# A transformer block with causal attention: shift rows and normalised outputs made by other engines, and TensorE's row halves taken in turn

## The chip, the cores and the metric

The kernel runs on one core of a Trainium2 chip. The metric is the device time of one execution in microseconds (us); the median of three runs of the kernel before is 739.92 us (739.89 to 741.77). A core has five engines that run their own instruction lists in order and meet by semaphores: TensorE (PE in the rows; PEld is its weight loading), VectorE (DVE), ScalarE (ACT), GpSimd (POOL) and SyncE (SP, which issues most transfers here). PSUM, where TensorE writes, has eight banks.

## The reference

For `x` of 4 x 1024 x 128:

```
x = x + 0.5 * ffn(layernorm(x))          # 8 experts of 64, 2 chosen, and a shared one
x = x + attention(layernorm(x))          # 16 heads of 8, 4 key heads, causal, slope bias
x = x + 0.5 * ffn(layernorm(x))
scores = q @ k.T * 8**-0.5 + slope * (key - query)     # -inf where key > query
out = softmax(scores) @ v
```

## The kernel before, in words

The first feed-forward part runs over 8 groups of 512 tokens; then comes attention in 16 **units** (one batch with one key head, four query heads), then the output projection (`out_proj`) and the second feed-forward part. The change lies in the attention and at its start and end.

A unit does two passes. **Pass 1** finds each query's largest score, so that the exponentials of pass 2 don't overflow. It is cut into 38 **pieces** (`PIECES`, numbered 0 to 37 here as in the code). A piece is one PSUM bank of scores with queries on the partitions: one product of up to 512 keys, or, where the causal part is narrow, a **merged** piece of two or four products and two products that add the causal mask (`per` over 1). Heads 0 and 1 of a unit lie on partitions 0 to 63, heads 2 and 3 on 64 to 127, so each product uses 57 or 59 rows of one **half** of the array. Even pieces use one half, odd pieces the other. VectorE reduces each piece to its maxima (`reduce`, L903, or L894 and L896 where a mask is added). The pieces go through a **ring** of three PSUM banks (`RING`): TensorE may write piece n only when what lay three places before it in the ring has been read (`slot`).

When pieces 0 to 11 are reduced, and again when all 38 are, `maxima` (L914) makes two bf16 rows from the 16 maxima per partition: the negative of the maximum, rounded, and what the rounding lost. TensorE transposes them (`maxima_T`, L1172, its row in the trace is L1175), VectorE copies them out (`rows_out`, L907), and SyncE moves them beside the queries (`load_maxima`), where they subtract the maximum as two more rows of the product.

**Pass 2** has 12 **steps** (one block of 128 keys with 512 queries). For each step TensorE makes scores with keys on the partitions (`score`, two head slots of two heads, one on each half of the array, and masks on the diagonal), ScalarE takes the exponential (`attention` of ACT, L624), and two steps later (`LAG`) TensorE multiplies by the values and a column of ones (`times_v`), four heads beside one another in bank `OBANK`. After 4 and after 12 steps ScalarE copies that bank out (`out_evac`, L613), TensorE transposes it back into the ring (`out_T`, L1178, helper L1023), and VectorE divides by the sum of the row (`normalise`, L935: a reciprocal, L940, and a multiplication, L941).

Pass 1 of unit i+1 runs between the steps of unit i. The order on TensorE is written by hand: `PER_STEP[s]` says how many pieces stand before the scores of step s+1, behind each of its two head slots, and behind `times_v`; `maxima_T(i, 1)` stands at the end of step 0, `out_T(i-1, 1)` of step 4, `maxima_T(i+1, 0)` of step 5, `out_T(i, 0)` of step 6. VectorE takes everything in the same order as the ring. GpSimd has little to do in attention: `load_v` (L520) once per unit and `add_bo` (L514) in the first eight. In the last unit there is no pass 1.

Of the kernel before, what the change touches and what calls it, by code (L numbers as in the profile page):

```python
# [8 lines left out]
ALU = mybir.AluOpType  # L9
# [3 lines left out]
P = 128  # L13
# [56 lines left out]
PER_STEP = [(2, 1, 0, 0), (0, 1, 1, 0), (0, 2, 2, 1), (0, 2, 0, 0), (0, 3, 0, 0), (0, 2, 0, 1),  # L70
# [11 lines left out]
LAG, PR_BUFS = 2, 5  # L82

# [92 lines left out]
def macaron(nc, dram, out):  # L176
    ctx = ExitStack()
    with ctx:
# [26 lines left out]
        mhalf = sb("mhalf", [P, GT])  # L205
        wg = sb("wg", [P, HT, P])
# [49 lines left out]
        mm_ = sb("mm_", [P, QT, HPG])  # L256
        wb = sb("wb", [P, 2, 2, SLOTS, QT], BF16)
# [3 lines left out]
        rden = sb("rden", [P, QT * HPG])  # L261
        attn = sb("attn", [P, UNITS, SEQ // P, HPG * DH])
# [52 lines left out]
        a_w = sem("a_w")  # L315
        a_wc = sem("a_wc")
# [4 lines left out]
        a_ov = sem("a_ov")  # L321
        a_on = sem("a_on")
# [141 lines left out]
        def _(pool):  # L464
            pool.memset(mhalf[:, :], -0.5)
            pool.memset(ones[:, :], 1.0)
# [54 lines left out]

            def values_and_bo(i, par, first, last):
                if not last:
                    load_v(i + 1, 1 - par)
                if i < BO_PARTS:
                    add_bo(i)

            pool.wait_ge(f1.v, GROUPS)
            load_v(0, 0)
            over_units(values_and_bo)  # L530
# [7 lines left out]
        def _(act):  # L538
# [75 lines left out]

            def attention():
# [16 lines left out]
                out_evac(UNITS - 1, 1)  # L632

# [17 lines left out]
        def _(dve):  # L651
# [231 lines left out]
            def reduce(i, n):  # L883
                t, h, per, k0, w, diag = PIECES[n]
                done = NP1 * i + n + 1
                b, at = ring.take(a_out, done)
# [18 lines left out]
            links = Chain(dve, a_ch)  # L905

# [7 lines left out]
            def maxima(i, j):  # L914

                dve.wait_ge(a_out, NP1 * i + (NP1 if j else FIRST_HALF))
                m = mx[:, 0, 0]
                if j:
                    m = mm_[:, :, :]
                    links.link(dve.tensor_tensor(m, mx[:, 1, 0], mx[:, 1, 1], V.max))  # L920
                after(dve, a_wc, 2 * i + j)
                m = m.rearrange("p t (r s) -> p r s t", r=2)
                links.link(dve.tensor_scalar(wb[:, :, 0, :, :], m, -1.0, None, V.mult))  # L923
                dve.scalar_tensor_tensor(out=wb[:, :, 1, :, :], in0=m, scalar=-1.0, in1=wb[:, :, 0, :, :],
                                         op0=V.mult, op1=V.subtract).then_inc(a_w, 1)

            def early_maxima(some):

                for n in some:
                    reduce(0, n)  # L930
                    if n == FIRST_HALF - 1:
                        maxima(0, 0)

            def attention(last_split):
                def normalise(i, j):  # L935
                    b, at = ring.take(a_on, 2 * i + j + 1)
                    after(dve, a_on, 2 * i + j)
                    dve.wait_ge(a_in, at + 1)
                    o = bank(b).rearrange("p (m e) -> p m e", m=QT * HPG)
                    links.link(dve.reciprocal(rden[:, :], o[:, :, DH]))  # L940
                    dve.tensor_tensor(  # L941
                        attn[:, i, QT * j:QT * j + QT, :].rearrange("p t (h d) -> p (t h) d", h=HPG),
                        o[:, :, 0:DH], rden[:, :, None].broadcast_to([P, QT * HPG, DH]), V.mult)\
                       .then_inc(a_on, 1)

# [4 lines left out]
                maxima(0, 1)  # L950
                START_LINKS = 3
                UNIT_LINKS = 2 + 3

                def body(i, par, first, last):

                    links.at(START_LINKS + UNIT_LINKS * i - (0 if first else 1))
                    for s in range(NSTEP):
                        if not last:
                            for n in range(part(s, 0).start, part(s, 3).stop):
                                reduce(i + 1, n)  # L960
                                if n == FIRST_HALF - 1:
                                    maxima(i + 1, 0)
                        if s == W1_STEP:
                            rows_out(i, par, 1)
                        if s == OT1_STEP and not first:
                            normalise(i - 1, 1)
                        if s == OT0_STEP:
                            normalise(i, 0)
                        if s == W0_STEP and not last:
                            rows_out(i + 1, 1 - par, 0)  # L970
                    if not last:
                        maxima(i + 1, 1)

                over_units(body)
                normalise(UNITS - 1, 1)
# [40 lines left out]
        def _(pe):  # L1016
# [63 lines left out]
            def ffn_down(f, qkv):  # L1080
                def early_pieces(some):
                    for n in some:
                        if n == 0:
                            pe.wait_ge(a_ld[0][0], 16 * LOADS)
                            pe.wait_ge(s_ks0, 4)
                        if n == SECOND_STACK:
                            pe.wait_ge(a_ld[1][0], 16 * LOADS)
                        piece(0, n)
# [65 lines left out]
            def piece(i, n):  # L1154
# [4 lines left out]
                b = slot(a_out, NP1 * i + n + 1)  # L1159
                for k in range(per):  # L1160
                    half, h = k // SLOTS, h0 % SLOTS + k % SLOTS
                    q0, key0 = (t + QT * half) * P, k0 + HALF * half
                    ins = mm(ps[:, b, k * w:k * w + w], qs[at:at + K1, par, q0 // HALF, h, q0 % HALF:q0 % HALF + P],
                             ks[at:at + K1, par, key0:key0 + w], start=k == 0, stop=per == 1)
                if per > 1:
                    o = ps[:, b, 0:per * w].rearrange("p (s n) -> p s n", s=per)
                    mask = mask_qk[at:at + RG, :, None, :].broadcast_to([RG, 2, per, P])
                    mm(o[:, :, w - P:w], spread[at:at + RG, 0, :], mask[:, 0], start=False)
                    ins = mm(o[:, :, w - RG:w], spread[at:at + RG, 1, :], mask[:, 1, :, RG:P], start=False)
                ins.then_inc(a_in, 1)  # L1170

# [187 lines left out]
```

## Time and profile before

| | |
|---|---|
| median of the runs | 739.92 us |
| the profiled execution's own time, and its span | 740.43 us, 738.6 us |
| PE busy, PEld busy | 702.6 us (95%), 365.6 us (50%) |
| DVE busy | 582.3 us (79%) |
| ACT busy, POOL busy | 403.3 us (55%), 112.6 us (15%) |
| the page's chain that ended last | PE 52%; DVE 13%; issue 11%; ACT 2% |
| TensorE's granted clock, mean | 0.972 |

Attention's full units lie between about 190 and 575 us of the span, the last one up to 600. Shares are averages over stages with different limits, so the units are read by themselves. In a timeline a row is one or more like instructions of one engine: start, length, what they are, how many, and in brackets how long the engine sat idle before and what released it. Records overlap where an engine is pipelined.

### The profile page before, as it was taken

Reading aid. Unit: us, or ns where it says so; the run is one execution under the profiler, and the core shown is the slowest. Engines: PE = TensorE matmul, PEld = TensorE weight load, DVE = VectorE, ACT = ScalarE, POOL = GpSimd, SP = SyncE. Lnnn points to the kernel's source line nnn. Section 1 sums busy time; section 2 is a strip of 40 time slices with the busy share of each in tenths; the row PEclk is TensorE's granted clock in tenths of the full one; section 3 lists DMA queues with packets and bytes.
Section 4 is the critical chain, followed back from the end, with each engine's and each line's share of the span. In section 5 each row is a group of like instructions: output and inputs, shape, how many; then the busy total and the mean of one; then the engine's idle time right before and its main releaser. Section 6 shows DMA issues by size and latency. Waiting matters only on the chain.

```text
span 738.6 us, 15927 instructions
## 1 busy us (share of the span) xinstructions
PE 702.6 (95%) x5906; PEld 365.6 (50%) x5906; DVE 582.3 (79%) x1921; ACT 403.3 (55%) x579; POOL 112.6 (15%) x122
## 2 busy tenths in 40 slices
PE   8999998967999999999999999999999889999998
PEld 4554487833344444444444444444444255554598
DVE  6976468697999999999999999999999238766311
ACT  3353332132667777776777777677777743353300
POOL 3202882110000000000000000000000002103950
PEclk9999999975899999999999999999999999999999
DMA  8014533442010011001100100110010000005531
GB/s 217 1 16 77 93 64 113 144 139 85 25 38 26 27 26 40 20 21 38 33 26 20 39 20 22 39 38 20 21 39 1 2 1 0 2 1 91 107 92 58
DMA packets 47249, 34.69 MB, mean 47 GB/s; under 512 B 13106, under 2 KB 46514, under 8 KB 47172
## 3 DMA queue, kind: packets, MB, share of 16 engines
q1 hardware_dynamic: 46596, 33.60, 18.6%
q8 instruction: 47, 0.77, 0.4%
q14 instruction: 30, 0.25, 0.1%
q10 hardware_dynamic: 576, 0.08, 0.1%
HBM read 23.01 MB, written 10.39 MB: 45 GB/s over the span
## 4 chain that ended last, share of the span: by engine, by line
PE 52%; DVE 13%; issue 11%; ACT 2%; DVEq 0%; ACTq 0%
PE ps L1018 49%; DVE mx L903 8%; PE ps L1023 4%; DVE mx L896 1%; ACT h_all L624 1%; DVE h_all L896 1%; DVE xn L705 1%; DVE stats L693 0%; DVE wb L923 0%; DVE mm_ L920 0%; DVE sg L838 0%; ACT osb L613 0%; DVE idle L894 0%; DVEq L133 0%; DVE mv L697 0%
## 5 line engine op out<-in xcount | busy, mean ns | idle before, releaser
L624 ACT ACTIVATE h_all<-ps 128x1024 f32<-128x1024 f32 (+3 forms) x384 | 291.3, 810 | 112.4 <-PE ps L1018 109.2
L903 DVE TENSOR_REDUCE mx<-ps 128x1 f32<-128x512 f32 (+2 forms) x352 | 223.0, 681 | 9.2 <-PE ps L1018 5.8
L1018 PE MATMUL ps<-ks,xnT_all 57*128 57x512 bf16 (+3 forms) x768 | 178.9, 337 | 15.6 <-DVE mx L896 6.4
L1018 PE MATMUL ps<-h_all,vb 128*32 128x512 f32 (+3 forms) x1536 | 163.8, 500 | 0.6 <-ACT osb L613 0.6
L1018 PE MATMUL ps<-xnT_all,ks 59*128 59x512 bf16 (+3 forms) x768 | 158.6, 331 | 3.6 <-ACT h_all L624 3.4
L896 DVE CUSTOM_DVE_ANT_0 h_all<-ps,mask_w 128x384 bf16<-128x384 f32 (+1 forms) x256 | 149.3, 618 | 2.3 <-issue 0.7
L1018 PEld LDWEIGHTS ps<-ks,xnT_all 57*128 57x128 bf16 x768 | 56.5, 94 | 143.4 <-DVE mx L896 64.9
L1018 PE MATMUL ps<-cb 64*128 64x64 bf16 (+3 forms) x1216 | 113.0, 215 | 0.0
L717 DVE TENSOR_TENSOR h_all<-ps,sg 128x512 f32<-128x512 f32 x80 | 55.2, 690 | 50.5 <-PE ps L1018 48.8
L563 ACT ACTIVATE sg<-ps 128x512 f32<-128x512 f32 x80 | 47.8, 597 | 82.6 <-PE ps L1018 82.3
L1018 PEld LDWEIGHTS ps<-cb 64*128 64x128 bf16 x1216 | 80.1, 96 | 17.3 <-issue 0.7
L1018 PE MATMUL ps<-xnT_all,wg 128*128 128x512 f32 x160 | 83.3, 602 | 0.0
L1018 PE MATMUL ps<-xnT_all,wu 128*128 128x512 f32 x160 | 81.7, 592 | 0.0
L1018 PE MATMUL ps<-wds,h_all 128*128 128x128 f32 x640 | 76.0, 279 | 0.0
L1018 PEld LDWEIGHTS ps<-wds,h_all 128*128 128x128 f32 x640 | 74.0, 194 | 2.7 <-issue 2.7
L1018 PEld LDWEIGHTS ps<-xnT_all,ks 59*128 59x128 bf16 x768 | 45.0, 93 | 42.8 <-ACT h_all L624 26.0
L520 POOL COPY vb<-v_all 128x64 f32<-128x64 f32 x16 | 3.7, 238 | 376.4 <-PE ps L1018 362.0
L1018 PEld LDWEIGHTS ps<-h_all,vb 128*32 128x32 f32 x1536 | 30.5, 108 | 38.1 <-issue 29.2
L1018 PEld LDWEIGHTS ps<-xnT_all,wu 128*128 128x128 f32 x160 | 30.4, 190 | 38.3 <-issue 38.0
L480 POOL TENSOR_TENSOR rstd<-ve,mhalf 128x4 f32<-128x4 f32 x24 | 24.2, 1009 | 151.6 <-DVE ve L699 145.0
L1018 PEld LDWEIGHTS ps<-xnT_all,wg 128*128 128x128 f32 x160 | 28.9, 190 | 28.7 <-issue 28.7
L858 DVE TENSOR_TENSOR x<-x,ps 128x512 f32<-128x512 f32 x16 | 10.9, 683 | 34.0 <-PE ps L1018 34.0
(120 smaller groups left out, 553.6 us busy)
## 6 DMA issues: line engine op xcount, KB each, us to landing
xnT_all<-q_scr SPq DMA_DIRECT2D x64, 96.0 KB
attn<-sel_scr SPq DMA_DIRECT2D x12, 256.0 KB, 7.2
mask_second<-sel_scr SPq DMA_DIRECT2D x12, 256.0 KB, 8.2
q_scr<-qp SPq DMA_DIRECT2D x8, 384.0 KB
ks<-k_scr SPq DMA_DIRECT2D x64, 48.0 KB
x<-in_x SPq DMA_DIRECT2D x8, 256.0 KB, 5.7
yT<-sel_scr SPq DMA_DIRECT2D x8, 256.0 KB, 9.0
q_scr<-qp SPq DMA_DIRECT2D x8, 256.0 KB
```

Source lines behind the costliest of these rows:

```text
L480: pool.tensor_tensor(rstd[:, par, :], ve[:, par, :], mhalf[:, :], ALU.pow).then_inc(rs_sem, 1)
L520: pool.tensor_copy(vb[:, par, :, 0:DH], v_all[:, i, :, :]).then_inc(a_vb, 1)
L563: act.activation(sg[:, b, :], bank(3 + b), ACT.Silu).then_inc(f.sg, 1)
L624: act.activation(pr[:, (NSTEP * i + s) % PR_BUFS, p:HPG:SLOTS, lo:HALF], ps[:, b:b + 2, lo:HALF], ACT.Exp)\
L705: ins = dve.tensor_scalar(xn[:, t, :], x[:, c * GT + t, :], mv[:, par, t, 0:1], rstd[:, par, t:t + 1], V.subtract, V.mult)
L717: dve.tensor_tensor(h_all[:, TILE_ORDER[k][0], TILE_ORDER[k][1], :], bank(5 + b), sg[:, b, :], V.mult)\
L858: dve.tensor_tensor(xt(c), xt(c), y, V.add).then_inc(f.x, 1)
L896: dve.tensor_tensor_reduce(out=junk, in0=ps[:, b, 0:w], in1=mask_w[:, HALF - w:HALF], scale=1.0, scalar=LOWEST, op0=V.add, op1=V.max, accu ...
L903: dve.tensor_reduce(m, src, AX.X, V.max).then_inc(a_out, 1)
L1018: return pe.matmul(o, l, r, start=start, stop=stop, skip_group_check=True)
L1023: ins = pe.transpose(ps[:, b, t * P:(t + 1) * P], src(t), ident)
```

## The change

- `maxima` leaves VectorE. GpSimd makes the rows (`shift_rows`: a multiplication by -1, a copy to bf16, a subtraction). For the second half VectorE still takes the maximum of two sets (`second_maxima`).
- `normalise` leaves VectorE. ScalarE copies 9 columns of each of 16 groups from the ring's bank to `raw` (`out_copy`, in steps 5 and 7, after the second exponential), and GpSimd raises the sums to the power -1 and multiplies. ScalarE's copy now empties that bank of the ring.
- Two merged pieces that stand next to one another in one group are issued as a pair (`two_pieces`): both banks are waited for first, then the products alternate between the halves of the array.
- The scores of a step begin with the half that the piece before them did not use.
- `PER_STEP[5]` changes, so that pieces 16 and 17 stand together, behind `times_v`.
- `maxima_T`, `out_T` and the steps keep their places.

```diff
-PER_STEP = [..., (0, 2, 0, 1),
+PER_STEP = [..., (0, 1, 0, 2),
...
@@ GpSimd
+            def normalise(i, j):
+                n = 2 * i + j + 1
+                pool.wait_ge(a_oc, n)
+                pool.tensor_tensor(rden[:, :], raw[:, j, :, DH], mone[:, :], ALU.pow).then_inc(a_rd, 1)
+                pool.wait_ge(a_rd, n)
+                pool.tensor_tensor(attn[...], raw[:, j, :, 0:DH], rden[...].broadcast_to(...), ALU.mult).then_inc(a_on, 1)
+                pool.wait_ge(a_on, n)
             def values_and_bo(i, par, first, last):
                 if not last:
                     load_v(i + 1, 1 - par)
                 if i < BO_PARTS:
                     add_bo(i)
+                if not last:
+                    shift_rows(i + 1, 0)
+                if not first:
+                    normalise(i - 1, 1)
+                normalise(i, 0)
+                if not last:
+                    shift_rows(i + 1, 1)
+                else:
+                    normalise(i, 1)
+            def shift_rows(i, j):
+                links = 2 * (2 * i + j)
+                m = mx[:, 0, 0]
+                if j:
+                    pool.wait_ge(a_mm, i + 1)
+                    m = mm_[:, :, :]
+                else:
+                    pool.wait_ge(a_out, NP1 * i + FIRST_HALF)
+                after(pool, a_wc, 2 * i + j)
+                pool.tensor_tensor(nm[:, :, :], m, mone.rearrange(...), ALU.mult).then_inc(a_nm, 1)
+                pool.wait_ge(a_nm, links + 1)
+                less = nm.rearrange("p t (r s) -> p r s t", r=2)
+                pool.tensor_copy(wb[:, :, 0, :, :], less).then_inc(a_nm, 1)
+                pool.wait_ge(a_nm, links + 2)
+                pool.tensor_tensor(wb[:, :, 1, :, :], less, wb[:, :, 0, :, :], ALU.subtract).then_inc(a_w, 1)
...
@@ ScalarE
+            def out_copy(i, j):
+                n = turned[i, j]
+                act.wait_ge(a_in, n)
+                after(act, a_on, 2 * i + j - 1)
+                act.activation(raw[:, j, :, :], bank((n - 1) % RING)...[:, :, 0:DH + 1], copy).then_inc(a_oc, 1)
...
+                            if p == 1 and s == OT1_STEP + 1 and not first:
+                                out_copy(i - 1, 1)
+                            if p == 1 and s == OT0_STEP + 1:
+                                out_copy(i, 0)
...
@@ VectorE
-            def maxima(i, j):
-                ...
-                def normalise(i, j):
-                    ...
+            def second_maxima(i):
+                dve.wait_ge(a_out, NP1 * (i + 1))
+                after(dve, a_w, 2 * i)
+                dve.tensor_tensor(mm_[:, :, :], mx[:, 1, 0], mx[:, 1, 1], V.max).then_inc(a_mm, 1)
...
@@ TensorE
+            def two_pieces(i, n):
+                upper, lower = slot(a_out, NP1 * i + n + 1), slot(a_out, NP1 * i + n + 2)
+                for first, second in zip(piece_products(i, n, upper), piece_products(i, n + 1, lower)):
+                    pass
+                first.then_inc(a_in, 1)
+                second.then_inc(a_in, 1)
+                RowsUsed.last = PIECES[n + 1][1] // SLOTS
...
             def score(i, s, p, par):
-                for r in range(2):
+                order = (1 - RowsUsed.last, RowsUsed.last)
+                for r in order:
```

How instructions move at the three places of which the prediction speaks:

TensorE, step 5 of a unit. `xnT_all,ks` are scores of pass 2, `ks,xnT_all` products of pieces, `cb` the mask products of a merged piece, `h_all,vb` is `times_v`, `cb,wb` is `maxima_T`. Before:

```order
L1018 MATMUL ps<-xnT_all,ks 128x512 x2
L1018 MATMUL ps<-ks,xnT_all 128x512
L1018 MATMUL ps<-ks,xnT_all 128x256 x2
L1018 MATMUL ps<-cb 128x2x128
L1018 MATMUL ps<-cb 128x2x64
L1018 MATMUL ps<-xnT_all,ks 128x512 x2
L1018 MATMUL ps<-h_all,vb 32x128 x4
L1018 MATMUL ps<-ks,xnT_all 128x256 x2
L1018 MATMUL ps<-cb 128x2x128
L1018 MATMUL ps<-cb 128x2x64
L1175 MATMUL ps<-cb,wb 32x128
```

And with the change:

```order
L1072 MATMUL ps<-xnT_all,ks 128x512 x2
L1072 MATMUL ps<-ks,xnT_all 128x512
L1072 MATMUL ps<-xnT_all,ks 128x512 x2
L1072 MATMUL ps<-h_all,vb 32x128 x4
L1072 MATMUL ps<-ks,xnT_all 128x256 x4
L1072 MATMUL ps<-cb 128x2x128 x2
L1072 MATMUL ps<-cb 128x2x64 x2
L1257 MATMUL ps<-cb,wb 32x128
```

Piece 16 has moved from before the second scores and `times_v` to behind them, and its five instructions alternate with those of piece 17.

VectorE, from piece 10 to piece 17 of a unit (steps 3 to 5), where `maxima` and `normalise` stood. Before:

```order
L903 TENSOR_REDUCE mx<-ps 128x2x2 [waits a_in] x2
L923 TENSOR_SCALAR wb<-mx 128x2x8 [waits a_wc,a_out]
L924 SCALAR_TENSOR_TENSOR wb<-mx,wb 128x2x8 [waits a_ch]
L903 TENSOR_REDUCE mx<-ps 128x1 [waits a_in] x3
L940 RECIPROCAL rden<-ps 128x16 [waits a_in,a_on]
L941 TENSOR_TENSOR attn<-ps,rden 128x128 [waits a_ch]
L903 TENSOR_REDUCE mx<-ps 128x1 [waits a_in]
L903 TENSOR_REDUCE mx<-ps 128x2 [waits a_in] x2
L912 COPY wt<-ps 32x128 [waits a_wd_first,a_in]
```

And with the change:

```order
L985 TENSOR_REDUCE mx<-ps 128x2x2 [waits a_in] x2
L985 TENSOR_REDUCE mx<-ps 128x1 [waits a_in] x4
L985 TENSOR_REDUCE mx<-ps 128x2 [waits a_in] x2
L992 COPY wt<-ps 32x128 [waits a_wd_first,a_in]
```

The reduces of pieces 10 to 17 now follow one another with nothing between.

GpSimd, one of the first eight units. Before:

```order
L520 COPY vb<-v_all 128x8x8 [waits a_pv]
L514 TENSOR_TENSOR x<-x,bo 128x512
```

And with the change:

```order
L541 TENSOR_TENSOR x<-x,bo 128x512
L585 TENSOR_TENSOR nm<-mx,mone 128x16 [waits a_wc,a_out]
L588 CAST wb<-nm 128x2x8 [waits a_nm]
L590 TENSOR_TENSOR wb<-nm,wb 128x2x8 [waits a_nm]
L553 TENSOR_TENSOR rden<-raw,mone 128x16 [waits a_oc]
L555 TENSOR_TENSOR attn<-raw,rden 128x128 [waits a_rd]
L553 TENSOR_TENSOR rden<-raw,mone 128x16 [waits a_oc,a_on]
L555 TENSOR_TENSOR attn<-raw,rden 128x128 [waits a_rd]
L585 TENSOR_TENSOR nm<-mm_,mone 128x16 [waits a_wc,a_mm,a_on]
L588 CAST wb<-nm 128x2x8 [waits a_nm]
L590 TENSOR_TENSOR wb<-nm,wb 128x2x8 [waits a_nm]
```

GpSimd has ten instructions more per unit, in one line with the two that it had.

## Rows read from the trace of the kernel before

**Rows 1.** Busy time by engine, units 1 to 7 (length, PE, PEld, DVE, ACT, POOL, clock, DMA):

```profile
199.60:399.50 199.90, 196.40 (x2174) 85.35 (x2175) 192.23 (x630) 149.08 (x205) 10.43 (x15) 1.00 0.11 29
```

**Rows 2.** The instructions on tile mm_: one per unit, ns min/median/max, first and last start:

```profile
L920 DVE TENSOR_TENSOR mm_<-mx x16: 174/175/176, 189.3 to 574.9; 128x16 f32<-128x16 f32 x16
```

**Rows 3.** Timeline of DVE: a wait, then piece 0, piece 12 of the next unit:

```profile
310.16 1.89 DVE L903 TENSOR_REDUCE mx<-ps 128x1 f32<-128x512 f32 x3 [0.28 <-PE ps L1018]
...
317.88 0.17 DVE L920 TENSOR_TENSOR mm_<-mx 128x16 f32<-128x16 f32 x1
...
318.40 1.28 DVE L903 TENSOR_REDUCE mx<-ps 128x2 f32<-128x512 f32 x2
...
325.66 0.17 DVE L923 TENSOR_SCALAR wb<-mx 128x16 bf16<-128x16 f32 x1
...
326.14 1.29 DVE L903 TENSOR_REDUCE mx<-ps 128x1 f32<-128x512 f32 x2
```

**Rows 4.** The chain that ended last, one unit (start, length, what):

```profile
321.37 0.03 DVE h_all L896
...
321.99 5.12 PE ps L1018 x46
...
329.74 0.70 DVE mx L903
...
330.49 2.37 PE ps L1018 x14
```

**Rows 5.** Timeline of PE: pieces 0 and 1, maxima_T, pieces 5 and 6, pieces 12 to 14:

```profile
317.52 0.40 PE L1018 MATMUL ps<-ks,xnT_all 57*128 57x256 bf16 x4
...
319.13 0.23 PE L1175 MATMUL ps<-cb,wb 128*32 128x128 bf16 x1
...
321.00 0.38 PE L1018 MATMUL ps<-ks,xnT_all 57*128 57x512 bf16 x2
...
325.73 0.59 PE L1018 MATMUL ps<-ks,xnT_all 57*128 57x512 bf16 x3
```

**Rows 6.** Timeline of PE, step 5: times_v, the start of piece 17:

```profile
328.79 0.43 PE L1018 MATMUL ps<-h_all,vb 128*32 128x128 f32 x8
329.15 0.39 PE L1018 MATMUL ps<-ks,xnT_all 57*128 57x256 bf16 x2
```

**Rows 7.** Timeline of DVE, steps 4 and 5: normalise, pieces 15 to 17:

```profile
327.95 0.25 DVE L940 RECIPROCAL rden<-ps 128x16 f32<-128x16 f32 x1
...
328.44 2.00 DVE L903 TENSOR_REDUCE mx<-ps 128x1 f32<-128x512 f32 x3
```

**Rows 8.** Groups by line and shape, ACT in attention (busy us, mean ns, idle before):

```profile
L624 ACT ACTIVATE h_all<-ps 128x256 f32<-128x256 f32 x60 | 21.5, 384 | 15.6 <-PE ps L1018 15.5
```

**Rows 9.** Timeline of ACT, exponentials of steps 6 and 8, which follow the two copies:

```profile
328.12 1.02 ACT L624 ACTIVATE h_all<-ps 128x1024 f32<-128x1024 f32 x1 [0.19 <-PE ps L1018]
...
334.11 1.03 ACT L624 ACTIVATE h_all<-ps 128x1024 f32<-128x1024 f32 x1 [1.48 <-PE ps L1018]
```

**Rows 10.** Groups by line and shape, POOL in the whole program:

```profile
L480 POOL TENSOR_TENSOR rstd<-ve,mhalf 128x4 f32<-128x4 f32 x24 | 24.2, 1009 | 151.6 <-DVE ve L699 145.0 <-issue 6.6
...
L514 POOL TENSOR_TENSOR x<-x,bo 128x512 f32<-128x512 f32 x8 | 10.1, 1264 | 0.0
...
L1353 POOL MEMSET const-float32-1.0<- 128x1 f32 x1 | 0.1, 99 | 0.0
```

**Rows 11.** Timeline, all engines, end of attention:

```profile
600.02 0.26 DVE L940 RECIPROCAL rden<-ps 128x16 f32<-128x16 f32 x1 [9.25 <-PE ps L1023]
...
600.73 0.76 DVE L982 COPY sg<-attn 128x512 f32<-128x512 f32 x2
...
601.21 1.09 PE L1023 MATMUL ps<-c,sg 128*128 128x128 f32 x8 [1.30 <-DVE sg L982]
```

**Rows 12.** Busy time by engine, start of the output projection:

```profile
601.20:604.00 2.80, 2.54 (x21) 2.30 (x22) 0.97 (x3) 1.09 (x2) 0.00 (x0) 1.00 0.00 0
```

**Rows 13.** Busy time by engine where TensorE waits for VectorE before attention (the clock is third from last):

```profile
164.00:191.30 27.30, 20.25 (x84) 8.22 (x84) 22.20 (x64) 6.34 (x9) 1.63 (x3) 0.50 0.25 75
```

More of the change, by code:

```diff
@@ L82, with turned_outputs @@
 LAG, PR_BUFS = 2, 5
+def turned_outputs():
+    n = NP1 + 1
+    numbers = {}
+    for i in range(UNITS):
+        for s in range(NSTEP):
+            n += sum(PER_STEP[s]) if i + 1 < UNITS else 0
+            n += s == W1_STEP
+            if s == OT1_STEP and i > 0:
+                numbers[i - 1, 1] = n = n + 1
+            if s == OT0_STEP:
+                numbers[i, 0] = n = n + 1
+            n += s == W0_STEP and i + 1 < UNITS
+    numbers[UNITS - 1, 1] = n + 1
+    return numbers
 BO_PARTS = 8
@@ L261, in macaron @@
         rden = sb("rden", [P, QT * HPG])
+        raw = sb("raw", [P, 2, QT * HPG, DH + 1])
         attn = sb("attn", [P, UNITS, SEQ // P, HPG * DH])
@@ L613, in out_evac @@
                 act.activation(osb[:, j, :], bank(OBANK), copy).then_inc(a_ov, 1)
+            turned = turned_outputs()
+            def out_copy(i, j):
+                n = turned[i, j]
+                act.wait_ge(a_in, n)
+                after(act, a_on, 2 * i + j - 1)
+                act.activation(raw[:, j, :, :], bank((n - 1) % RING).rearrange("p (m e) -> p m e", m=QT * HPG)[:, :, 0:DH + 1],
+                               copy).then_inc(a_oc, 1)
             def attention():
@@ L885, in reduce @@
                 done = NP1 * i + n + 1
+                if n == 0:
+                    after(dve, a_w, 2 * i - 1)
                 b, at = ring.take(a_out, done)
@@ L965, in body @@
                         if s == OT1_STEP and not first:
-                            normalise(i - 1, 1)
+                            ring.take(a_oc, 2 * i)
                         if s == OT0_STEP:
-                            normalise(i, 0)
+                            ring.take(a_oc, 2 * i + 1)
                         if s == W0_STEP and not last:
@@ L1081, in early_pieces @@
                 def early_pieces(some):
[L1082 to L1088, printed above, removed]
+                    if 0 in some:
+                        pe.wait_ge(a_ld[0][0], 16 * LOADS)
+                        pe.wait_ge(s_ks0, 4)
+                    if SECOND_STACK in some:
+                        pe.wait_ge(a_ld[1][0], 16 * LOADS)
+                    pieces_of(0, some)
                 def down(c, par, transpose=False):
@@ L1152, in slot, with piece_products @@
                 return b
-            def piece(i, n):
+            class RowsUsed:
+                last = 1
+            def piece_products(i, n, b):
                 t, h0, per, k0, w, diag = PIECES[n]
@@ L1194, in score @@
                     for half, w in enumerate((RG, P)):
-                        for r in range(2):
+                        for r in order:
                             rows = slice(RG * r, RG * r + RG)
@@ L1221, in attention @@
                 pe.wait_ge(a_ld[1][0], 16 * LOADS)
-                for n in range(EARLY_END + sum(TAIL), NP1):
-                    piece(0, n)
+                pieces_of(0, range(EARLY_END + sum(TAIL), NP1))
                 pe.wait_ge(a_wd[0], 32)
@@ L1229, in pieces @@
                     def pieces(s, k):
-                        for n in () if last else part(s, k):
-                            if n == 0:
-                                next_stack(i, par, 0)
-                            if n == SECOND_STACK:
-                                next_stack(i, par, 1)
-                            piece(i + 1, n)
+                        some = range(0) if last else part(s, k)
+                        if 0 in some:
+                            next_stack(i, par, 0)
+                        if SECOND_STACK in some:
+                            next_stack(i, par, 1)
+                        pieces_of(i + 1, some)
                     for s in range(NSTEP):
```

71 lines of the change are left out of this document (35 added, 36 removed).

## The prediction

> **What bounds the kernel now.** I read the busy shares first, stage by stage. In units 1 to 7 VectorE is busy 192.23 of 199.90 us, 96%, with TensorE's clock at 1.00 [rows 1]. TensorE's 196.40 is no better guide to who limits whom, since the modelled ends of its matmuls overlap with waits. `mm_` is made once per unit, and its first and last starts give the period: (574.9 - 189.3) / 15 = 25.71 us [rows 2]. A quick reader stops here: VectorE is full, so whatever leaves it is gained. The views after that speak against it. VectorE has gaps, and they end with TensorE: 0.28 us before piece 26's reduce [rows 3]. And the chain that ended last, followed through a unit, goes from the reduce at 321.37 through 5.12 us of TensorE, comes back at the reduce of piece 17 at 329.74, and leaves through 2.37 us of TensorE from 330.49 [rows 4]. No instruction of `normalise` stands on it. VectorE limits the unit at a few reduces only, and each of these begins when its piece is ready. So each place where work is removed has to be asked for itself: is the next piece there earlier?
>
> **What leaves VectorE, per unit.** Four stretches go. The two row instructions at the unit's end: from `mm_` at 317.88 to piece 0 at 318.40 are 0.52, of which the `mm_` part, which stays, holds about 0.21 (its 0.17 and a gap), so 0.31. The rows after piece 11: 326.14 - 325.66 = 0.48 [rows 3]. `normalise` in step 4: 328.44 - 327.95 = 0.49 [rows 7], and the second one of the same two instructions, about as much. Together 1.77 us; over the 15 units with a pass 1 that is 26.6 us, if all of it paid.
>
> I price each by the piece behind it, adding 0.37 us from a product's issue to its reduce (pieces 5 and 6 issue at 321.00, piece 5's reduce begins at 321.37 [rows 4, 5]).
> - *Unit's end, 0.31.* Pieces 0 to 4 come 0.31 earlier, but pieces 5 and 6 are issued at 321.00 whatever VectorE does: they stand behind scores that wait for the exponentials of the step before. Piece 5's reduce began the moment it was ready. The 0.31 becomes a gap: nothing.
> - *After piece 11, 0.48.* Piece 12 is issued at 325.73 [rows 5], ready at 326.10; it was reduced at 326.14 [rows 3]. Gain 0.04.
> - *`normalise` in step 4, 0.49.* Pieces 15 and 16 could follow up to 0.2 us earlier, but piece 17's products start at 329.15, behind `times_v` at 328.79 [rows 6]; it sets the reduce at 329.74, which is on the chain [rows 4].
> - *`normalise` in step 6, about 0.5.* VectorE waits for TensorE soon after it already [rows 3]; the wait grows by what leaves.
>
> **What the change adds or moves.**
> - *Piece 16 behind `times_v`.* Its products take 0.39 [rows 6] and leave the stretch before `times_v`, which moves from 328.79 to 328.40 at best. The pair then starts where the last of the values leaves the array, 328.75, and has products of 0.39 and masks to do: ready about 329.30. VectorE, done with piece 15 at about 328.9, stands idle until then, takes 16 (0.6) and begins 17 at 329.93 instead of 329.74. That is on the chain: +0.2 per unit, 15 x 0.2 = +3.0. Bounds 0 (piece 17's reduce stays where it is) and +0.3.
> - *Order by halves.* Four 256-column products on both halves take 0.40 [rows 5], two on one half 0.39 [rows 6]: the halves already run beside one another, in the program order of before. Taking them in turn finds nothing left to overlap: 0.
> - *ScalarE's copies.* The nearest row is its 128x256 at 384 ns [rows 8]; 144 columns are an estimated 0.29. The first follows the exponentials of step 5; before step 6's next one ScalarE had waited 0.19 [rows 9], so 0.1 shows, and the copy of `OBANK` behind it waits for `times_v` anyway. The second falls into a wait of 1.48 [rows 9]. Cost 0; without the covers 15 x 0.58 = 8.7.
> - *GpSimd's rows.* Three operations of 16 columns. The nearest rows are 99 ns for one column and 1264 for 512, which puts 16 columns at about 0.13 [rows 10]; with a handover each I take 0.9 us for the chain against 0.43 on VectorE. `maxima_T` runs at 319.13 [rows 5], and `mm_` is ready at 318.05 [rows 3], so it is in time, barely. Cost 0; upper bound in the rivals.
> - *GpSimd's division in the loop* has over 10 us until anyone wants the bank of `raw`: 0.
> - *Before attention* the first rows leave VectorE in a stretch where TensorE waits for it [rows 13]: -0.3 (0 to -0.5).
>
> **The tail.** After the last unit nothing covers the division. Before: reciprocal at 600.02, gathering copy at 600.73, so 0.71; TensorE idles 1.30 [rows 11]. With the change: ScalarE's copy 0.29, the power of 16 columns, the product of 128 columns (about 0.39 by the same line), three handovers of 0.08. The power is the uncertain one. A power of 4 columns costs 1009 ns against 99 for nearly nothing [rows 10], so 0.23 per column if it is paid by column: 0.10 + 16 x 0.23 = 3.7. If the 1.01 is a fixed price, 1.0. I take 3.7, because an addition of 512 columns is only 0.25 dearer than this power of 4: what costs is the power, and each element has one. Tail: 0.29 + 3.73 + 0.39 + 0.24 = 4.65, minus 0.71 = +3.9 (bounds +1.2 and +4.3).
>
> TensorE then idles 5.2 us instead of 1.3. Where it waited often for VectorE, the granted clock was 0.50, the 1.2 GHz level [rows 13]; I expect it to fall here too. The first 2.80 us of the projection hold 2.54 of TensorE [rows 12]: at half clock up to +2.5, with none +0; I take +1.3.
>
> **The sum** against the profiled execution: 740.43 + 3.0 + 3.9 + 1.3 - 0.3 = 748.3. The median of the runs lies 0.5 below that execution, so **748 us**. With the terms' own bounds the forecast runs from 743 to 752.
>
> **Rivals.** What a measurement can tell here is about 0.3%, that is 2.2 us: "same" is 737.7 to 742.1.
> - *VectorE does set the period* (25%). Its 96% speaks for it [rows 1], as do the chain's VectorE links: if the scores that I hold fixed are late only because an earlier ring bank was late, everything slides forward together and the removed time is paid out. Full: 740.4 - 26.6 - 0.3 + 5.2 - 0.5 = 718; it decides for faster from a third of 26.6, and I give 716 to 737. Against it stands that pieces 5, 12 and 17 were each reduced within 0.04 us of being ready.
> - *Halves only overlap when alternated* (5%). If products on different halves could not run past one another out of turn, each pair would save about 0.4, and the three pairs of a unit 1.2: 15 x 1.2 = 18 less, without piece 16's price 727. The pieces 0 and 1 at 0.40 for four products [rows 5] speak against it. The Trainium skill, TensorE: Matmul & The Clock Gate, section Part 3: Packing small matmuls, states that matmuls start and end strictly in program order, which would make the alternation worth something. By that rule it is 727; the trace disagrees with it at these rows, so the sum goes by the trace.
> - *Nothing in the units, and a cheap power* (11%): the tail costs 1.2, the clock stays: 738 to 742.
> - *GpSimd is late with the rows* (7%). If each small operation costs the 1.01 of the nearest small row, the chain is 3.0 + 0.2 and `maxima_T`, at 321.3 instead of 319.5 at the latest, holds all TensorE's work behind it: +1.7 per unit, +25, 755 to 775. It decides from about 0.4 us per operation. Against it: the interpolation above.
>
> **Chances.** The forecast's case (743 to 752) gets 52%. Faster: the first two rivals but their least gains, 29%; same 12%; slower 59%. For 8 in 10 the range must reach into the first rival: 726 to 753; the likeliest case's own range is 743 to 752.
>
> **What would show it.** Right: the period from `mm_` is 25.7 to 25.95; VectorE's busy share in units 1 to 7 falls to about 90% and its new waits end with TensorE; a gap stands before piece 16's reduce; the power of 16 columns takes about 3.7; from the last `out_T` to the first gathering copy are over 5 us; the clock is under 1.00 near 605 us. Wrong: a period of 25 us or less, VectorE's share still above 94% (the first rival), products of a pair in 0.4 where before each had its own (the second), a power near 1 us, or `maxima_T` waiting for GpSimd (the last).

## The result, and the profile after

The changed kernel takes 748.76 us (median of 5 runs, 746.75 to 749.42) against 739.92 (739.46 to 741.77). The ratio is 1.011, with a 95% interval of 1.0089 to 1.0132: slower by 1.1%. The forecast was 748, from a range of 726 to 753. The sum nearly met the number; two of its terms, and two that it didn't have, still need telling. All stretches below are from the profiled executions, whose spans are 738.6 and 747.0 us, so 8.4 us apart.

First the stretch of [rows 1] in the changed kernel, busy time by engine (it is nearly eight units long, not the seven of its heading):

```profile
199.60:399.50 199.90, 192.20 (x2135) 77.73 (x2133) 180.69 (x556) 150.70 (x215) 69.56 (x89) 1.00 0.10 29
```

VectorE went from 192.23 to 180.69 us, from 96% to 90%, and yet the unit is longer. Where the free time lies, the waits of VectorE in the same stretch show, before and then after (what waited, for what, us in total, times, longest):

```profile
DVE mx L903 <- PE ps L1018: 2.7, 11, 0.3
```

```profile
DVE mx L985 <- PE ps L1072: 13.5, 46, 0.6
DVE h_all L978 <- issue: 3.8, 15, 0.3
```

VectorE waits for TensorE's pieces, 13.5 us instead of 2.7. The instructions on `mm_`, as in [rows 2], and two of them in the timeline of VectorE:

```profile
L998 DVE TENSOR_TENSOR mm_<-mx x16: 174/175/176, 189.0 to 580.8; 128x16 f32<-128x16 f32 x16
```

```profile
217.78 0.18 DVE L998 TENSOR_TENSOR mm_<-mx 128x16 f32<-128x16 f32 x1
...
580.78 0.17 DVE L998 TENSOR_TENSOR mm_<-mx 128x16 f32<-128x16 f32 x1
```

From first to last the period looks like (580.8 - 189.0) / 15 = 26.12 us. But the first unit alone is 217.78 - 189.0 = 28.8; the other 14 take (580.78 - 217.78) / 14 = 25.93 each. Before, the first was 25.79 and the others 25.71. From here on "period" means the 14 units after the first, read in this way, and times "after `mm_`" are counted from a unit's `mm_`.

The 0.22 us of such a unit show at step 5. Timeline of VectorE at pieces 15 to 18, to be held against [rows 7]:

```profile
331.94 0.69 DVE L985 TENSOR_REDUCE mx<-ps 128x1 f32<-128x512 f32 x1 [0.24 <-PE ps L1072]
333.00 1.29 DVE L985 TENSOR_REDUCE mx<-ps 128x2 f32<-128x512 f32 x2 [0.37 <-PE ps L1072]
334.21 0.20 DVE L992 COPY wt<-ps 32x128 bf16<-32x128 bf16 x1
334.34 0.67 DVE L985 TENSOR_REDUCE mx<-ps 128x1 f32<-128x512 f32 x1
```

And TensorE there, with `times_v`, then the pair of pieces 16 and 17:

```profile
332.05 0.43 PE L1072 MATMUL ps<-h_all,vb 128*32 128x128 f32 x8
332.41 0.39 PE L1072 MATMUL ps<-ks,xnT_all 57*128 57x256 bf16 x4
332.64 0.33 PE L1072 MATMUL ps<-cb 64*128 64x256 bf16 x4
```

`normalise` is gone and VectorE is done with piece 15 at 332.63; then it stands for 0.37 us, since the pair's products start at 332.41, behind `times_v`. Piece 17 is reduced 0.61 after piece 16, at 333.61. Before it was 329.74, 11.86 after its unit's `mm_` at 317.88; now 333.61 - 321.49 = 12.12. The chain that ended last passes through just this place:

```profile
333.01 0.06 DVE mx L985
...
333.61 0.69 DVE mx L985
...
334.35 2.36 PE ps L1072 x14
```

Then the end of attention, all engines, as in [rows 11]:

```profile
604.23 0.29 ACT L687 ACTIVATE raw<-ps 128x144 f32<-128x144 f32 x1 [0.81 <-PE ps L1077]
604.66 2.90 POOL L553 TENSOR_TENSOR rden<-raw,mone 128x16 f32<-128x16 f32 x1 [6.16 <-ACT raw L687]
607.64 0.41 POOL L555 TENSOR_TENSOR attn<-raw,rden 128x128 f32<-128x128 f32 x1
608.08 0.76 DVE L1036 COPY sg<-attn 128x512 f32<-128x512 f32 x2 [25.55 <-POOL attn L555]
...
608.57 1.97 PE L1077 MATMUL ps<-c,sg 128*128 128x128 f32 x8 [4.37 <-DVE sg L1036]
```

The power of 16 columns takes 2.90 us. TensorE idles 4.37 us instead of 1.30, and the eight products after it take 1.97 us instead of 1.09. That is the clock, as the rows from 607.50 on show. Busy time by engine at four places of the changed kernel (the clock is third from last): the start of the first unit, a stretch of the last unit, and the start of the projection in two parts:

```profile
189.00:199.60 10.60, 10.60 (x85) 4.29 (x80) 7.46 (x30) 6.45 (x10) 2.04 (x5) 0.54 0.01 3
```

```profile
585.00:592.50 7.50, 5.49 (x50) 1.48 (x42) 0.00 (x0) 6.26 (x9) 2.24 (x1) 1.00 0.00 1
```

```profile
607.50:610.00 2.50, 1.44 (x7) 1.44 (x8) 1.04 (x3) 0.28 (x1) 0.47 (x2) 0.66 0.00 0
610.00:613.00 3.00, 3.00 (x21) 2.77 (x20) 0.97 (x3) 1.30 (x3) 0.00 (x0) 0.72 0.00 0
```

And the first two stretches in the kernel before:

```profile
189.00:199.60 10.60, 10.19 (x108) 4.13 (x105) 9.79 (x38) 8.47 (x12) 0.00 (x0) 0.89 0.01 3
585.00:592.50 7.50, 6.00 (x42) 1.97 (x42) 0.55 (x2) 5.23 (x7) 0.00 (x0) 0.77 0.01 2
```

So the 8.4 us are made of these (each a difference of two distances between the same events of both traces):

| stretch | before | after | difference |
|---|---|---|---|
| start to the first `mm_` | 189.27 | 189.01 | -0.26 |
| first unit | 25.79 | 28.77 | +2.98 |
| 14 units | 359.88 | 363.00 | +3.12 |
| last `mm_` to the last `out_T` | 24.35 | 22.78 | -1.57 |
| last `out_T` to the first gathering copy | 1.44 | 4.52 | +3.08 |
| from there to the end | 137.83 | 138.89 | +1.06 |

### The profile page after: what moved, and what is told of

Read it like the earlier page. It is cut to its first block, busy times and chain, and to the rows that moved or that the text cites. A ratio compares the mean times of both kernels' runs of the same rounds, so it can differ in the third digit from the quotient of the medians.

```text
span 747.0 us, 16052 instructions
## 1 busy us (share of the span) xinstructions
PE 702.3 (94%) x5906; PEld 356.3 (48%) x5906; DVE 562.1 (75%) x1793; ACT 410.9 (55%) x611; POOL 239.8 (32%) x283
## 4 chain that ended last, share of the span: by engine, by line
PE 62%; issue 7%; DVE 7%; ACT 2%; POOL 0%; DVEq 0%; ACTq 0%; POOLq 0%
PE ps L1072 58%; PE ps L1077 4%; DVE mx L985 3%; ACT h_all L699 2%; DVE mx L978 1%; DVE xn L785 1%; POOL rden L553 0%; DVE stats L773 0%; DVE h_all L978 0%; DVE sg L918 0%; ACT osb L679 0%; DVE idle L976 0%; DVE mv L777 0%; DVE qp L921 0%; DVE x L938 0%
## 5 line engine op out<-in xcount | busy, mean ns | idle before, releaser
L1072 PE MATMUL ps<-ks,xnT_all 57*128 57x512 bf16 (+3 forms) x768 | 173.9, 339 | 17.7 <-DVE mx L985 9.6
L1072 PE MATMUL ps<-xnT_all,ks 59*128 59x512 bf16 (+3 forms) x768 | 154.5, 332 | 5.5 <-ACT h_all L699 3.5
L978 DVE CUSTOM_DVE_ANT_0 h_all<-ps,mask_w 128x384 bf16<-128x384 f32 (+1 forms) x256 | 151.2, 619 | 10.7 <-issue 9.2
L1072 PEld LDWEIGHTS ps<-ks,xnT_all 57*128 57x128 bf16 x768 | 52.2, 94 | 152.5 <-DVE mx L978 66.0
L553 POOL TENSOR_TENSOR rden<-raw,mone 128x16 f32<-128x16 f32 x32 | 93.0, 2905 | 78.9 <-ACT raw L687 78.9
L1072 PE MATMUL ps<-cb 64*128 64x64 bf16 (+3 forms) x1216 | 104.6, 216 | 0.0
L1072 PEld LDWEIGHTS ps<-cb 64*128 64x128 bf16 x1216 | 74.9, 97 | 16.7 <-issue 0.4
L1072 PEld LDWEIGHTS ps<-xnT_all,ks 59*128 59x128 bf16 x768 | 43.3, 93 | 45.5 <-ACT h_all L699 31.7
L507 POOL TENSOR_TENSOR rstd<-ve,mhalf 128x4 f32<-128x4 f32 x24 | 24.2, 1007 | 104.4 <-DVE ve L779 97.7
L520 POOL TENSOR_TENSOR h_all<-h_all,attn 128x512 f32<-128x512 f32 x24 | 27.0, 1159 | 68.2 <-DVE h_all L797 35.5
```

The costliest lines, as they stand in the source:

```text
L507: pool.tensor_tensor(rstd[:, par, :], ve[:, par, :], mhalf[:, :], ALU.pow).then_inc(rs_sem, 1)
L520: pool.tensor_tensor(h_all[:, c, tiles, :], h_all[:, c, tiles, :], expert_mask[b][:, tiles, :], ALU.mult).then_inc(f.hm, 1)
L553: pool.tensor_tensor(rden[:, :], raw[:, j, :, DH], mone[:, :], ALU.pow).then_inc(a_rd, 1)
L978: dve.tensor_tensor_reduce(out=junk, in0=ps[:, b, 0:w], in1=mask_w[:, HALF - w:HALF], scale=1.0, scalar=LOWEST, op0=V.add, op1=V.max, accu ...
L1072: return pe.matmul(o, l, r, start=start, stop=stop, skip_group_check=True)
```

## The experiments

The period is read from one profile each and repeats within 0.02 us from unit to unit. Runs whose loops are the same agree: the changed kernel and four at 25.93, six and eleven at 25.38, two, five and nine at 25.65 to 25.66. So effects of 0.05 us per unit show in it, which a time alone could not tell. Ratios are against the kernel before.

**One: step 5 undone.** In the changed kernel:

```diff
-            (0, 3, 0, 0), (0, 1, 0, 2),
+            (0, 3, 0, 0), (0, 2, 0, 1),
```

> The change with PER_STEP[5] as it was: piece 16 stands before times_v again, alone, all else as changed. My theory (piece 16 behind times_v makes the 0.22 us that a unit has become longer): the period from the mm_ starts falls from 25.93 to 25.70 to 25.78 us, piece 17's reduce stands 11.8 to 12.0 us after mm_, the time falls by 2.5 to 3.5 us to about 745.5. Rival (the longer unit comes from the pairs, the order of the scores or the copies of ScalarE): the period stays at 25.9. Rival (VectorE sets the period and the move hid its gain): 25.2 or less, about 738.

Measured: period 25.74, piece 17's reduce 11.93 after `mm_`, 743.4 us, ratio 1.0042 (1.0029 to 1.0056). Moving piece 16 behind `times_v` makes 0.18 of the 0.22 (with its pair with piece 17, which is undone too). The median fell by 5.4 us, more than was expected and more than the 2.7 of 15 units. In the profiles the rest lies where the clock comes and goes: this run's first unit took 25.88 us and not 28.77, the way to it was 1.2 shorter, and the last unit was 1.6 longer. The part on the prediction comes back to that.

**Two: the offloading alone.** Step 5 undone, no pairs, scores in a fixed order:

```diff
-            (0, 3, 0, 0), (0, 1, 0, 2),
+            (0, 3, 0, 0), (0, 2, 0, 1),
...
-                    together = n + 1 < some.stop and ...
+                    together = False
...
-                order = (1 - RowsUsed.last, RowsUsed.last)
+                order = range(2)
```

> The change without any of its parts on TensorE: PER_STEP[5] as it was, no pairs, scores always in the order half 0, half 1; VectorE still gives its 1.8 us per unit away. My theory (VectorE's time stands beside other work): period 25.65 to 25.75, like before's 25.71, and the time is before's plus the end of attention (3 to 4 us) and up to 3 us of clock, 743 to 747. Rival (VectorE sets the period): up to 1.8 us per unit come out, 25.2 or less, 716 to 737.

Measured: period 25.66, 742.58 us, a little under the expected 743 to 747, ratio 1.0026 (1.0014 to 1.0038). Busy time in the stretch of [rows 1], and VectorE at pieces 15 to 17:

```profile
199.60:399.50 199.90, 195.61 (x2178) 83.70 (x2175) 182.82 (x573) 152.64 (x220) 69.81 (x90) 1.00 0.10 29
```

```profile
328.00 1.29 DVE L985 TENSOR_REDUCE mx<-ps 128x1 f32<-128x512 f32 x2 [0.24 <-PE ps L1072]
329.48 0.69 DVE L985 TENSOR_REDUCE mx<-ps 128x2 f32<-128x512 f32 x1 [0.18 <-PE ps L1072]
```

This is the cleanest test of the argument that VectorE's 96% was not the bound. VectorE gives 1.8 us per unit away, counted from start to start, and the unit is 0.05 shorter. (Its busy time falls by 1.25, from 24.72 to 23.47 per unit: the records of reduces that follow one another overlap, and where one now waits they don't.) Pieces 15 and 16 come 0.17 to 0.18 earlier, and then VectorE waits 0.18 for piece 17. The first rival of the prediction falls here.

**Three: the order alone.** In the kernel before:

```diff
-            (0, 3, 0, 0), (0, 2, 0, 1),
+            (0, 3, 0, 0), (0, 1, 0, 2),
```

> The kernel before with the new PER_STEP[5] alone: VectorE, ScalarE and GpSimd as before. My theory (TensorE's order makes the loss): the period rises from 25.71 to 25.9 to 26.0, since the gap before piece 16 would be filled by what VectorE still has to do, and the time to 743 to 744.5. Rival (the loss comes from handing the work over to ScalarE and GpSimd): 25.71.

Measured: period 25.90, 743.39 us in one run. VectorE does its `normalise` here and still waits for piece 16:

```profile
329.33 0.29 DVE L941 TENSOR_TENSOR attn<-ps,rden 128x128 f32<-128x128 f32 x1
329.54 0.68 DVE L903 TENSOR_REDUCE mx<-ps 128x1 f32<-128x512 f32 x1
330.44 1.29 DVE L903 TENSOR_REDUCE mx<-ps 128x2 f32<-128x512 f32 x2 [0.22 <-PE ps L1018]
```

So the move costs 0.19 per unit by itself, with none of the handing over and without pairs.

**Four: gathering copies that wait only for what they read.** In the changed kernel, before the copies of batches 0, 1 and of each later one, and on TensorE before the first transposition of the projection:

```diff
-                dve.wait_ge(a_on, 2 * UNITS)
+                dve.wait_ge(a_on, 2 * KVH)
                 gather(0, 0, 0, 0)
                 gather(1, 0, 1, 1)
+                dve.wait_ge(a_on, 2 * KVH * 2)
                 gather(2, 1, 0, 0)
...
                 for b in range(1, BATCH - 1):
+                    dve.wait_ge(a_on, 2 * KVH * (b + 2))
...
+                pe.wait_ge(a_oc, 2 * UNITS)
                 attention_T(0, 0)
```

> The change, with the gathering copies of the output projection waiting only for the units that they read, so that the first of them need not wait for the last unit's division on GpSimd; TensorE waits for ScalarE's copy of the last bank instead. My theory (the end of attention costs 3.1 us of waiting for the power and 1.05 us of clock after it): TensorE's idle time at that place falls from 4.37 to about 0.5 us, the clock stays at 1.00 there, the time falls by 4 to 5.5 us to about 744. Rival (the division's time is hidden or only moves to the later gathering copies): less than 1.5 us.

Measured: 742.45 us, ratio 1.0022 (1.0007 to 1.0037). The end of attention, all engines, and the clock behind it:

```profile
602.76 0.29 ACT L687 ACTIVATE raw<-ps 128x144 f32<-128x144 f32 x1 [0.81 <-PE ps L1079]
...
603.10 1.09 PE L1079 MATMUL ps<-c,sg 128*128 128x128 f32 x8 [0.38 <-ACT raw L687]
603.19 2.90 POOL L553 TENSOR_TENSOR rden<-raw,mone 128x16 f32<-128x16 f32 x1 [6.15 <-ACT raw L687]
```

```profile
603.10:608.00 4.90, 4.65 (x38) 4.24 (x39) 2.67 (x5) 2.07 (x4) 3.31 (x2) 1.00 0.00 0
```

TensorE idles 0.38 instead of 4.37, the power runs beside the projection, and the clock stays at 1.00, with 1.09 us for the eight products. From the last `out_T` to these products it is 1.01 us instead of 5.01, so 4.0, and 0.9 after that: 4.9, as expected. In the kernel before that way took 1.92, so 3.1 of the 4.0 undo the change's cost, and 0.9 are a gain that the kernel before could have had too; no run tries that. The medians differ by 6.3, more than the expected 4 to 5.5. The rest lies where the clock comes and goes again: the two programs are the same up to the last unit, and the period is 25.93 in both, but this run's first unit took 26.40 us and not 28.77, the way to it was 0.6 shorter, and from the last `mm_` to the last `out_T` it took 24.29 and not 22.78. The start of its first unit:

```profile
189.00:199.60 10.60, 9.88 (x104) 3.32 (x105) 9.60 (x33) 8.48 (x12) 2.45 (x7) 0.94 0.01 2
```

The mean clock there is 0.94; in the changed kernel's profile it was 0.54.

**Five to eight: an order that uses the free time.** If TensorE's order is what holds the unit, freed VectorE time should pay once the order asks for it. Five, the offloading (as in two) with the early gathering copies (as in four):

> The offloading without the changed order on TensorE (as in the second experiment), with the early gathering copies of the fourth. My theory adds up: a period of 25.65 to 25.67, no wait for the power at the end, so 15 x 0.27 = 4 us less than with the early gathering copies alone (742.45): 738 to 739.5, no more than 0.3% under the kernel before. Rival (the two don't add up, the clock takes it back): 740 or more.

Measured: 737.44 us, ratio 0.996 (0.9946 to 0.9975), period 25.65. It adds up and is a little better than the expected 738, its first unit at 25.62 us. Six, on top of it, piece 17 ahead of `times_v`:

```diff
-            (0, 3, 0, 0), (0, 2, 0, 1),
+            (0, 3, 0, 0), (0, 2, 1, 0),
...
-                            if p == 0 and s == EV0_STEP:
+                            if p == 1 and s == EV0_STEP:
                                 out_evac(i, 0)
```

> The fifth kernel with PER_STEP[5] = (0, 2, 1, 0): piece 17 before times_v instead of behind it, and ScalarE's copy of OBANK behind the second exponential of step 6 instead of the first, so that the exponentials don't wait for the later times_v. My theory (the loop waits for TensorE's order at piece 17, and VectorE, freed, can take it earlier): piece 17's reduce at about 11.6 us after mm_ instead of 11.86, the period 25.35 to 25.50. Rival (some other link holds the unit): 25.6 or more.

Measured: period 25.38, piece 17's reduce 11.57 after `mm_`, 733.45 us in one run. ScalarE's copy moves with piece 17, and no run parts the two edits; the 0.27 that the unit gains is what piece 17's reduce gains (11.84 to 11.57). Seven, piece 5 as well:

```diff
-... (0, 1, 1, 0), (0, 2, 2, 1),
+... (0, 1, 1, 1), (0, 1, 2, 1),
```

> The sixth kernel with piece 5 also moved ahead, from behind the scores of step 3 to behind times_v of the step before (PER_STEP[1] = (0, 1, 1, 1), PER_STEP[2] = (0, 1, 2, 1)), so that VectorE's run of reduces 5 to 11 starts earlier. My theory: both shifts add up, period 25.1 to 25.3, time 731 to 735, below the kernel before by about 1%. Rival (VectorE's freed time is worth nothing in any order, TensorE's own work is the bound): 25.5 or more, 737 or more.

Measured: period 25.40, 733.05 us, ratio 0.9908 (0.9889 to 0.9928). Half of the theory failed: piece 5 early gains nothing. Its reduce does come 0.15 earlier, but the first exponential of step 3 starts 0.16 later, and piece 9's reduce 0.13 later. Eight, the same order in the kernel before, where VectorE keeps its work:

> The kernel before with the order of the seventh (pieces 5 and 17 early, the copy of OBANK behind the second exponential), but VectorE keeps its four stretches of 1.8 us per unit and waits at the end are as before. My theory (freed VectorE time pays only when TensorE's order offers it work): the gain is smaller than the seventh's, period 25.5 to 25.75, 737 to 741. Rival (the order alone does it): as the seventh, 25.1 to 25.3, about 733 to 735.

Measured: period 25.61, 737.13 us, ratio 0.9959 (0.9943 to 0.9974). That makes a table of four, period in us (the lower row has ScalarE's copy moved as well):

| | VectorE keeps its work | offloaded |
|---|---|---|
| order of before | 25.71 | 25.66 |
| pieces 5 and 17 early | 25.61 | 25.40 |

Alone they give 0.05 and 0.10, together 0.31. Timeline of VectorE in the sixth kernel at pieces 15 to 17:

```profile
327.11 1.89 DVE L985 TENSOR_REDUCE mx<-ps 128x1 f32<-128x512 f32 x3 [0.24 <-PE ps L1074]
```

The three reduces follow one another without the wait that stood before piece 17 in the second experiment. In eight, with `normalise` in VectorE's list, piece 15 starts 0.2 later than there and piece 17 with it.

**Nine and ten: what made the other 0.09.** The first experiment's unit is 0.09 longer than the second's. They differ by the pairs and by the order of the scores, so each is taken out of the first experiment alone. Nine, the pairs:

```diff
-                    together = n + 1 < some.stop and ...
+                    together = False
```

> The kernel of the first experiment (PER_STEP[5] as it was) with every piece issued by itself, the scores still beginning with the half that the piece before did not use. The first experiment's unit took 25.75 us, the offloading alone 25.66. My theory (the pair of pieces 10 and 11 waits for both banks of the ring before its first product, which costs 0.09 us): 25.65 to 25.67, piece 10's reduce back at 6.45 us after mm_. Rival (the order of the scores costs it): 25.75, with piece 10's reduce at 6.45 or at 6.77. The Trainium skill's rule of strict order, by which the pairs save 0.8 us per unit here: 26.3 or more.

Measured: period 25.65, piece 10's reduce 6.44 after `mm_` instead of 6.77. Up to piece 9 the reduces of both runs stand within 0.01 of one another; from piece 12 to the end of the unit those of the first experiment are 0.09 or 0.10 later. Ten, the order of the scores:

```diff
-                order = (1 - RowsUsed.last, RowsUsed.last)
+                order = range(2)
```

> The kernel of the first experiment with the scores always in the order half 0, half 1, and the pairs kept. My theory (the order of the scores is worth nothing): 25.73 to 25.77, as the first experiment. Rival (the order of the scores costs what the first experiment has over the offloading alone): 25.66. Rival (it saves what the pairs lose): 25.8 or more.

Measured: period 25.75. The order of the scores is worth nothing, and the pairs cost 0.09. TensorE at pieces 10 and 11 as a pair (first experiment), then VectorE there:

```profile
322.72 0.40 PE L1072 MATMUL ps<-ks,xnT_all 57*128 57x128 bf16 x8
322.94 0.51 PE L1072 MATMUL ps<-cb 64*128 64x512 bf16 x4
```

```profile
323.47 1.29 DVE L985 TENSOR_REDUCE mx<-ps 128x4 f32<-128x512 f32 x2 [0.25 <-PE ps L1072]
```

The same pieces one after the other (nine):

```profile
323.51 0.39 PE L1072 MATMUL ps<-ks,xnT_all 57*128 57x128 bf16 x4
...
323.83 0.34 PE L1072 MATMUL ps<-ks,xnT_all 57*128 57x128 bf16 x3
323.96 0.27 PE L1072 MATMUL ps<-cb 64*128 64x256 bf16 x1
```

```profile
324.33 1.28 DVE L985 TENSOR_REDUCE mx<-ps 128x4 f32<-128x512 f32 x2
```

The pair does alternate well: eight products in 0.40 us. But it starts 6.02 after `mm_` (322.72 - 316.70), where piece 10 alone starts at 5.62 (323.51 - 317.89). The pair waits for piece 11's bank too, which piece 8's reduce gives free at about 5.9; alone, piece 11 starts at 5.94 (323.83 - 317.89). What alternating wins, waiting together loses, and 0.09 more.

**Eleven: the best, timed.** The sixth kernel again:

> The sixth kernel once more, with rounds of timing (piece 17 early, the offloading, the early gathering copies, no pairs). My theory: a period of 25.38, and a time of 732 to 734.5, 0.8 to 1.1% below the kernel before, no slower than the seventh. Rival (its single time was a lucky one): above 735.

Measured: 733.52 us, ratio 0.9907 (0.9889 to 0.9925), period 25.38. It beats the kernel before by 0.9%, as the seventh does, with one edit less; between these two the intervals tell nothing apart. Of the 6.3 us between the medians the 14 units make 4.6 and the early gathering copies 0.9.

## Why the prediction was right, term by term

- *VectorE's 1.77 us per unit stand beside other work.* Right, and shown by two: 0.05 us of it came out per unit. The way it was found holds too: ask at each removed stretch when the next piece is ready, not how busy the engine is.
- *Piece 16 behind `times_v`, +0.2 per unit, +3.0.* Right: 0.19 alone in the kernel before (three), 0.18 in the changed one (one). The gap before piece 16 and piece 17's later reduce are in the rows.
- *Order by halves, 0.* Right for the scores. Wrong for the pairs: the sentence "taking them in turn finds nothing left to overlap: 0" asked only what alternation could win. It overlooked that the pair takes two banks at once. Pieces 10 and 11 start 0.4 late for that, and the unit loses 0.09 (nine), some 1.3 us in all. With the 0.05 gained and the 0.18 to 0.19 lost it makes the 0.22 that was measured. The prediction's 0.20 thus met the unit with two small errors of opposite sign.
- *ScalarE's copies and GpSimd's rows, 0.* Right. The copy takes 0.29. GpSimd's three operations take 0.22, 0.20 and 0.22 instead of 0.13, and their chain in the unit shown starts at 321.80 and is over at 322.59, before `maxima_T` at 322.74. Only once, before attention, did `maxima_T` wait for them, 2.4 us; the wait of 3.77 for a bank that followed it before is 0.66 now, and the start up to the first `mm_` comes out 0.26 shorter, near the -0.3 of the sum. That nearness is luck: over all profiles the first `mm_` stands at 189.00 to 189.27 where VectorE keeps its work and anywhere from 187.66 to 189.01 where it doesn't.
- *The tail, +3.9.* The mechanism was right, the size was off: +3.08. The power was put at 3.73, by the column; it takes 2.90. The 1009 ns for four columns was not all paid by the column: with two points, 1009 and 2902, it is about 0.16 per column and 0.38 besides.
- *The clock at the projection, +1.3.* +1.06, by the same mechanism. In all five profiles in which TensorE waited 4.37 us there (the changed kernel, one, two, nine, ten) the clock fell; in none of the eight with a wait of 0.38 or 1.30 did it. How much it cost differed: from the first products of the projection to the end three of the five took 138.36 to 138.50 us and two (two and nine) 139.81 and 139.85, against 137.33 to 137.53 where it stayed up. The second experiment at that place:

```profile
602.00:604.50 2.50, 2.50 (x11) 2.27 (x12) 0.69 (x2) 1.11 (x2) 0.00 (x0) 0.50 0.00 0
```

- *Missed: the clock in the first and the last unit,* +2.98 and -1.57. In the profile of the changed kernel it is still at its lower level for the first third of the first unit, to about 198.7. The prediction put all of the clock's price at the projection. But this isn't shown to be the change's doing. Six and eleven are one program, and their first units took 27.00 and 25.66 us; the changed kernel and four, the same up to the last unit, 28.77 and 26.40. Busy time and clock from the start of the first unit, in the changed kernel (two rows), in six and in eleven (two rows):

```profile
189.00:198.60 9.60, 9.60 (x77) 4.14 (x72) 6.46 (x29) 5.78 (x9) 2.04 (x5) 0.50 0.01 3
198.80:217.70 18.90, 18.08 (x188) 6.99 (x189) 16.77 (x45) 14.24 (x19) 3.97 (x5) 1.00 0.12 31
```

```profile
188.30:195.70 7.40, 7.40 (x60) 2.87 (x58) 5.55 (x25) 4.68 (x8) 2.05 (x5) 0.50 0.01 2
```

```profile
188.40:190.50 2.10, 2.10 (x20) 1.02 (x16) 1.84 (x5) 2.08 (x3) 1.72 (x5) 0.50 0.00 0
190.70:214.00 23.30, 22.76 (x243) 9.28 (x244) 21.36 (x67) 17.39 (x25) 4.08 (x6) 1.00 0.09 26
```

The place moves from run to run, and why it does was not tested. The timed runs tell what it is worth. Three runs of the changed kernel with a mean granted clock of 0.966 took 748.76 to 749.42 us, the two with 0.975 took 746.75 and 747.24. The kernel before, over all the runs beside the experiments, took 741.98 to 742.97 at 0.965 and 739.10 to 740.49 at 0.974 to 0.977. At a like clock the change thus costs 6 to 8 us, and the parts that are the change's own, 3.1 of the units, 3.1 of the tail and 1.1 at the projection, make 7.3.

That 748 came within 1 us of the median is in part luck. The prediction's terms make 7.9, which is 0.6 above these parts, mostly since the power was put too dear; the first and the last unit, for whose clock it had no term, added 1.4 in the profile.

Of the prediction's signs of being right, the period, VectorE's 90% with waits that end with TensorE, and the gap before piece 16 came. Three others didn't: the power took 2.90 and not 3.7, the way from the last `out_T` to the first gathering copy 4.52 and not over 5, and the clock was still 1.00 up to 607.5 and fell only when the wait was over or nearly so. One sign of being wrong, that of the second rival, showed: the products of pieces 16 and 17 take 0.39 together (332.41). It was badly chosen, since pieces 0 and 1 took 0.40 together already before [rows 5].

The rivals: "VectorE sets the period" fell in two. "Halves only overlap when alternated" fell in nine: with the pairs off the unit got shorter, and piece 11's first three products start at 323.83, ahead of piece 10's second mask product at 323.96, which stands before them in the program. The Trainium skill (TensorE: Matmul & The Clock Gate, section Part 3: Packing small matmuls) states that matmuls start and end strictly in order; these rows disagree with it for products on different halves. "Nothing in the units, and a cheap power" fell with the unit's 0.22 and the power's 2.90. GpSimd was not late in the units.

## What to carry to other kernels

An engine that is busy 96% of a stretch need not limit it: go to each piece of work that would be removed, and ask when the next one has its input. Time that is freed beside a chain paid here mostly with an order that asks for it (0.05 without, 0.31 with), so test the handing over and the new order apart and together. The slower engine cost nothing inside the loop and 3.1 us at its end, until whoever waited there waited only for what it read.

## What the runs showed of the hardware

- GpSimd's power takes 1007 ns for 128x4 and 2902 ns for 128x16, its small multiplications and casts of 16 columns 0.20 to 0.22 us. A multiplication of 128 columns takes 0.41.
- TensorE's clock after a stretch of waits came back at different places in runs of the same program: about 195.8 in six and 190.6 in eleven. The first unit of attention took 25.5 to 28.8 us over all profiles here, while the later units of a kernel agree within 0.02.
- With a wait of TensorE of 4.37 us at the end of attention the clock fell there in five profiles of five, with one of 0.38 or 1.30 in none of eight.
- Eight products of 128 columns, alternating between the halves of the array, take 0.40 us, four on one half 0.39. Products on one half start ahead of an earlier piece's masks on the other (323.83 and 323.96 in nine).
